# A chunked recurrence on one core: GpSimd's masked copies in one-input steps, the output norm at the end of its chunk, one transpose for two sources

## The reference

```python
def step(carry, inp):
    W1c, b1c = carry
    xq, xk, xv, et = inp
    Z1 = xk @ W1c + b1c
    grad = _ln_l2_bwd(Z1, xv - xk, g, bb)        # backward of a layer norm
    Attn1 = jnp.tril(xq @ xk.swapaxes(-1, -2))
    b1_bar = b1c - jnp.tril(et) @ grad
    Z1_bar = xq @ W1c - et * Attn1 @ grad + b1_bar
    last_eta = et[..., -1, :, None]
    W1n = W1c - (last_eta * xk).swapaxes(-1, -2) @ grad
    b1n = b1c - (last_eta * grad).sum(-2, keepdims=True)
    return ((W1n, b1n), xq + _ln(Z1_bar, g, bb, EPS_IN))
_, out = jax.lax.scan(step, (W1_0, b1_0), (chunk(XQ), chunk(XK), chunk(XV), eta))
x = x + L0(_gn(x));  x = x + L1(_gn(x))
```

## Time and profile before

| | |
|---|---|
| device time, median of 3 executions | 696.14 us (694.52 to 696.18) |
| the profiled execution's own time | 696.66 us |
| its span in the trace | 694.9 us |
| busy of the span: TensorE, weight load, VectorE, ScalarE, GpSimd | 76%, 53%, 71%, 48%, 54% |
| instructions on GpSimd | 660 |

### The profile page before, as it was taken

How to read it: one execution, slowest core, us unless ns; L and a number is a source line. 1 busy time by engine, 2 the same in 40 slices (tenths; PEclk the granted TensorE clock), 3 DMA queues, 4 the chain that set the end, 5 groups by cost and what they waited for, 6 DMA issues and landing times. The chain is left out here.

```text
span 694.9 us, 30768 instructions
## 1 busy us (share of the span) xinstructions
PE 528.8 (76%) x12150; PEld 368.1 (53%) x12150; DVE 491.4 (71%) x1547; ACT 331.6 (48%) x1044; POOL 377.8 (54%) x660
## 2 busy tenths in 40 slices
PE   0498999994577777777777777777773899669996
PEld 0143343434467666666666666666773345255542
DVE  6357676664588999999999999999995367434340
ACT  0434432224255555555555555555555576353422
POOL 0368788773365655655666556556664475402222
PEclk9999999996555555555555555555555899979987
DMA  9001111115600000000000000000001500001112
GB/s 349 36 18 39 34 30 31 30 41 121 145 4 0 0 0 0 0 0 0 0 0 0 0 0 0 0 0 0 0 4 42 218 0 0 1 18 62 52 42 90
DMA packets 9851, 24.56 MB, mean 35 GB/s; under 512 B 1845, under 2 KB 2510, under 8 KB 9550
## 3 DMA queue, kind: packets, MB, share of 16 engines
q1 hardware_dynamic: 9806, 24.01, 11.3%
HBM read 11.42 MB, written 4.19 MB: 22 GB/s over the span
## 5 line engine op out<-in xcount | busy, mean ns | idle before, releaser
L762 PE MATMUL PS<-work 32*32 32x32 f32 x4064 | 84.2, 238 | 76.1 <-DVE work L911 67.6
L762 PEld LDWEIGHTS PS<-work 32*32 32x32 f32 x4064 | 80.3, 152 | 86.2 <-issue 82.1
L963 POOL TENSOR_TENSOR work<-work,mask 128x256 f32<-128x256 f32 x64 | 46.7, 729 | 83.4 <-DVE work L911 70.6
L751 PE MATMUL PS<-work 64*32 64x64 f32 x2048 | 69.3, 310 | 19.3 <-ACT work L1006 17.1
L500 PE MATMUL PS<-X,work 128*128 (+3 forms) x160 | 72.1, 597 | 7.0 <-ACT X L640 6.4
L751 PEld LDWEIGHTS PS<-work 64*32 64x32 f32 x2048 | 55.6, 164 | 26.1 <-issue 24.8
L774 PE MATMUL PS<-work 32*64 32x32 f32 x2016 | 68.4, 292 | 0.6 <-issue 0.6
L774 PEld LDWEIGHTS PS<-work 32*64 32x64 f32 x2016 | 59.7, 216 | 4.8 <-issue 0.7
L1031 ACT ACTIVATE work<-PS,small 128x128 f32<-128x128 f32 x64 | 23.5, 367 | 80.1 <-PE PS L751 80.1
L1323 POOL TENSOR_TENSOR TT<-TT,KN 128x512 f32<-128x512 f32 x16 | 19.8, 1264 | 60.4 <-ACT TT L1454 60.2
L500 PEld LDWEIGHTS PS<-X,work 128*128 128x128 f32 (+1 forms) x160 | 25.9, 169 | 48.0 <-issue 47.1
(11 more groups left out here) (145 smaller groups left out, 1321.8 us busy)
## 6 DMA issues: line engine op xcount, KB each, us to landing
X<-in_x SPq DMA_DIRECT2D x4, 1024.0 KB, 8.1
KN<-KP SPq DMA_DIRECT2D x64, 64.0 KB, 1.9
X<-QP SPq DMA_DIRECT2D x8, 512.0 KB, 9.4
KN<-in_x SPq DMA_DIRECT2D x4, 1024.0 KB, 8.8
out<-TT SPq DMA_DIRECT2D x16, 256.0 KB, 2.2
work<-in_rope SPq DMA_DIRECT2D x2, 512.0 KB, 9.7
cst<-in_consts SPq DMA_DIRECT2D x1, 289.0 KB, 4.9
work<-in_wk SPq DMA_DIRECT2D x1, 256.0 KB, 11.1
```

The costliest lines, as they stand in the source:

```text
L751: mm = nc.tensor.matmul(PS[HD * a:HD * a + HD, ZB[p], b * ZW:b * ZW + ZW], KT2[p][r:r + 64, k * B + b, :, :].rearrange("p e t -> p (e t)") ...
L762: mm = nc.tensor.matmul(PS[HD * a:HD * a + HD, bank, b * width:b * width + HD], AM[p][HD * a:HD * a + HD, b, part, :, :].rearrange("p e t ...
L963: nc.gpsimd.tensor_tensor(AM[p].rearrange("p b s e t -> p (b s) e t"), S1[p].unsqueeze(2).broadcast_to([P, 2 * B, E, CS]), mask2.rearrange ...
```

## The change

The change is confined to the recurrence, apart from addresses. GpSimd's masked copies `KT2` and `KHX`, until now one two-input product each against a broadcast mask, become two one-input products each, with one column of the mask as the scalar. `out_norm(c-3)` moves from between `YL` and the wait for `GL` to the end of GpSimd's `body(c)`. The pair of variance and deviation `vq` gets two buffers. TT and KN become the halves of one tensor `TK`, so that VectorE's two transposes become one. GpSimd's chunks are all written out, where 56 of them ran in a loop. VectorE's `out_rows` with its wait is untouched.

```diff
-        KN = sb("KN", [P, J, NT])
-        TT = sb("TT", [P, J, NT])
+        TK = sb("TK", [P, J, 2, NT])
+        TT, KN = TK[:, :, 0, :], TK[:, :, 1, :]
...
-        vq = carve(2 * B)
-        var1, sdq = vq[:, 0:B], vq[:, B:2 * B]
+        vq = [carve(2 * B) for _ in range(2)]
+        var1, sdq = [v[:, 0:B] for v in vq], [v[:, B:2 * B] for v in vq]
...
                     if past(c, 2):
                         dve.wait_ge(q["khx"], c - 1)
-                    for s, src in enumerate((TT, KN)):
-                        tr = nc.vector.transpose(
-                            TKH[p][:, s, :, :].rearrange("p b d -> p (b d)"),
-                            src.rearrange("p e (b n) -> p b e n", b=B)[:, :, :, ds(c * CS, CS)])
-                    tr.then_inc(q["tkh"], 1)
+                    nc.vector.transpose(
+                        TKH[p].rearrange("p s b d -> p (s b d)"),
+                        TK[:, :, :, :].rearrange("p e s (b n) -> p (s b) e n", b=B)[:, :, :, ds(c * CS, CS)]
+                    ).then_inc(q["tkh"], 1)
...
                     if past(c, 2):
                         pool.wait_ge(q["base"], c - 1)
-                    nc.gpsimd.tensor_tensor(
-                        KT2[p], chunk(KP, c).unsqueeze(2).broadcast_to([P, J * B, E, CS]),
-                        ccol("emask_k").unsqueeze(1).unsqueeze(3).broadcast_to([P, J * B, E, CS]),
-                        ALU.mult).then_inc(q["kt2"], 1)
+                    for e in range(E):
+                        kt = nc.gpsimd.tensor_scalar(KT2[p][:, :, e, :], chunk(KP, c), ccol("emask_k", e, 1),
+                                                     None, ALU.mult)
+                    kt.then_inc(q["kt2"], 1)
...
-                    nc.gpsimd.tensor_tensor(
-                        KHX[p], TKH[p][:, 1, :, :].unsqueeze(2).broadcast_to([P, B, E, HD]),
-                        upd_mask.unsqueeze(1).unsqueeze(3).broadcast_to([P, B, E, HD]), ALU.mult
-                    ).then_inc(q["khx"], 1)
+                    for e in range(E):
+                        kx = nc.gpsimd.tensor_scalar(KHX[p][:, :, e, :], TKH[p][:, 1, :, :],
+                                                     upd_mask[:, e:e + 1], None, ALU.mult)
+                    kx.then_inc(q["khx"], 1)
...
                     nc.gpsimd.tensor_tensor(YL, YY[:, 0, :, :], bc(lead[:, 0, :]), ALU.mult).then_inc(q["yl"], 1)
-                    if past(c, 3):
-                        out_norm(c - 3, 1 - p)
                     pool.wait_ge(q["gl"], c + 1)
...
                     if not is_last(c):
                         khx(c + 1, 1 - p)
+                    if past(c, 3):
+                        out_norm(c - 3, 1 - p)
...
-                run_chunks(pool, body)
+                for c in range(NC):
+                    body(c, c % 2)
...
-                def out_sd(c):
+                def out_sd(c, p):
                     act.wait_ge(q["ssq"], c + 1)
-                    if past(c, 1):
-                        act.wait_ge(q["zn"], c + 0)
-                    nc.scalar.activation(sdq, ssq, ACT.Sqrt, bias=eps6, scale=1.0 / HD).then_inc(q["sdq"], 1)
+                    if past(c, 2):
+                        act.wait_ge(q["zn"], c - 1)
+                    nc.scalar.activation(sdq[1 - p], ssq, ACT.Sqrt, bias=eps6, scale=1.0 / HD).then_inc(q["sdq"], 1)
```

More of the change, by code:

```diff
@@ L851, in out_r @@
                     dve.wait_ge(q["sdq"], c + 1)
-                    nc.vector.reciprocal(sdq, sdq).then_inc(q["rq"], 1)
+                    o = 1 - c % 2
+                    nc.vector.reciprocal(sdq[o], sdq[o]).then_inc(q["rq"], 1)
                 def out_turn(c):
@@ L887, in body @@
                         dve.wait_ge(q["sdq"], c - 2)
-                        nc.vector.reciprocal(vq, vq).then_inc(q["r"], 1)
+                        nc.vector.reciprocal(vq[p], vq[p]).then_inc(q["r"], 1)
                     else:
-                        nc.vector.reciprocal(var1, var1).then_inc(q["r"], 1)
+                        nc.vector.reciprocal(var1[p], var1[p]).then_inc(q["r"], 1)
                     dve.wait_ge(q["ts"], c + 1)
@@ L970, in out_norm @@
                         pool.wait_ge(q["zt"], c + 0)
-                    nc.gpsimd.tensor_tensor(ZN, ZQ[p], bc(sdq), ALU.mult).then_inc(q["zn"], 1)
+                    nc.gpsimd.tensor_tensor(ZN, ZQ[p], bc(sdq[1 - p]), ALU.mult).then_inc(q["zn"], 1)
                 def body(c, p):
                     pool.wait_ge(q["r"], c + 1)
-                    nc.gpsimd.tensor_tensor(lead[:, 0, :], var1, lrh[:, ds(c, 1), :].squeeze(1), ALU.mult
+                    nc.gpsimd.tensor_tensor(lead[:, 0, :], var1[p], lrh[:, ds(c, 1), :].squeeze(1), ALU.mult
                                             ).then_inc(q["u"], 1)
                     pool.wait_ge(q["u"], c + 1)
-                    nc.gpsimd.tensor_tensor(lead[:, 1, :], var1, lead[:, 0, :], ALU.mult).then_inc(q["u2"], 1)
+                    nc.gpsimd.tensor_tensor(lead[:, 1, :], var1[p], lead[:, 0, :], ALU.mult).then_inc(q["u2"], 1)
                     pool.wait_ge(q["y"], c + 1)
                     nc.gpsimd.tensor_tensor(YL, YY[:, 0, :, :], bc(lead[:, 0, :]), ALU.mult).then_inc(q["yl"], 1)
-                    if past(c, 3):
-                        out_norm(c - 3, 1 - p)
                     pool.wait_ge(q["gl"], c + 1)
@@ L1058, in body @@
                         act.wait_ge(q["u2"], c + 0)
-                    nc.scalar.activation(var1, ss, ACT.Identity, bias=eps6, scale=1.0 / HD).then_inc(q["v"], 1)
+                    nc.scalar.activation(var1[p], ss, ACT.Identity, bias=eps6, scale=1.0 / HD).then_inc(q["v"], 1)
                     if past(c, 1):
@@ L1069, in body @@
                     if past(c, 2):
-                        out_sd(c - 2)
+                        out_sd(c - 2, p)
                     if past(c, 1):
@@ L1085, in _ @@
                 out_store(NC - 4)
-                out_sd(NC - 2)
+                out_sd(NC - 2, 0)
                 out_square(NC - 1, 1)
                 out_store(NC - 3)
-                out_sd(NC - 1)
+                out_sd(NC - 1, 1)
                 out_store(NC - 2)
@@ L1266, in build @@
             if at[1] + n > J * NT:
-                at = [flat(TT), 0]
+                at = [TT[:, 0, :], 0]
             DST.append(at[0][:, at[1]:at[1] + n].rearrange("p (r w) -> p r w", w=kept))
@@ L1273, in build @@
                for k, (r, w, _, kept) in zip((0, 1, 2, 0, 1), STAGES)]
-        YB = [flat(TT)[:, 4096 + s * 2048:4096 + (s + 1) * 2048].rearrange("p (k n) -> p k n", k=PER * J)
+        YB = [TT[:, 1, s * 2048:(s + 1) * 2048].rearrange("p (k n) -> p k n", k=PER * J)
               for s in range(2)]
```

## The result

The changed kernel takes 856.77 us (median of 4, 854.7 to 858.1) against 695.33 us for the kernel before, a ratio of 1.232 with a 95% interval of 1.228 to 1.235. It is slower, as forecast, but by 161 us, not by 86: the time lies 49 us above the range. It stands next to the rival in which each half costs as much as the whole, 858 us, to which I gave 6 in 100.

The account below looks back on a forecast made before the run. VectorE's program was taken as the bound, so new waits are paid in full. A chunk of 2.81 + 1.14 + 3.03 = 6.98 us against 5.55 gave 86.2 us more in all, so 782 us; range 766 to 808.

Parts of the forecast that it names:

- the rival in which each half costs as much as the whole: GpSimd's one-input steps each keep the halved product's 0.61 us through a fixed cost: 76 us more, 858 us; 6 in 100.
- The wait at `out_rows`: VectorE's `out_rows` waits for the moved norm, starting 2.81 us after the gradient instead of 0.63: about 2.2 us stall per chunk.
- the price of the one-input steps: GpSimd's four one-input steps per chunk each take 0.25 us to the next start, like the copy.
- The upper bound: A one-input step on GpSimd costs at most the same-size two-input product, 0.40 us, some 0.355 to the next start: +25 us.
- The part beside VectorE: From L874 to the next gradient VectorE takes 3.03 us instead of 3.48, as GpSimd is silent beside it.
- the written-out program: GpSimd starts its masks 0.37 us after the gradient instead of 0.51, counted within the wait; extra instruction fetch costs nothing.
- the single transpose: One VectorE transpose for two, between gradient and `out_rows`, is worth nothing with or without the new wait.
- the second buffer of the variances: ScalarE's `out_sd` waits for a norm one chunk older, off the path before and after: costs nothing.
- Nothing outside the recurrence: Changed addresses keep transfers' row lengths, so the stages outside the recurrence change by nothing.
- The rule on shared reads: A two-SBUF-input VectorE instruction and a GpSimd instruction reading SBUF exclude one another; without it the total is 27 us more.

Follow-up runs that it names:

- experiment 1: The changed kernel with the output norm back at its old place, ahead of the wait for the gradient: 687.59 us, ratio 0.988.
- experiment 8: The changed kernel with two-input products and the norm directly behind the masks, halfway between old and new place: 705.18 us, ratio 1.012.
- experiment 2: The changed kernel with each masked copy as one two-input product again, norm still at the end: 785.62 us, ratio 1.130.
- experiment 5: The changed kernel with eleven extra GpSimd instructions on scratch ahead of the recurrence, at 4, 128 or 256 elements: 859.81 us (one execution).
- experiment 6: The changed kernel with five extra GpSimd instructions ahead of the recurrence, of other operations, a strided view and a larger product: 857.43 us (one execution).
- experiment 7: The changed kernel with a second operation, an addition of 0.0, in each one-input step: 800.64 us, ratio 1.151.
- experiment 4: The kernel before with GpSimd's program written out and nothing else: 687.16 us, ratio 0.985.
- experiment 3: The changed kernel with the norm at its old place and two-input products: 684.52 us, ratio 0.984.
- experiment 9: The changed kernel with two-input products, a third buffer of ZQ and ScalarE's program written out, norm at the end: 687.27 us, ratio 0.985.
- experiment 10: The changed kernel with a third buffer of ZQ and ScalarE's program written out, one-input steps kept: 751.48 us, ratio 1.077.
- experiment 11: The changed kernel with two-operation one-input steps, third buffer of ZQ and ScalarE's program written out, norm at the end: 707.22 us, ratio 1.016.
- experiment 14: The changed kernel with third ZQ buffer, ScalarE written out, norm behind the masks, key blocks two-input, key rows one-input: 684.09 us, ratio 0.984.
- experiment 13: The changed kernel with the norm at its old place, key blocks one-input, key rows by a two-input product: 684.21 us, ratio 0.984.

## Why the prediction was right about the place and wrong about the size

*The wait at `out_rows`: right.* The wait that no row of before showed, with 1.28 us to spare, became 3.49 us of idle time in each chunk, released by L971, and in the last two chunks `out_rows` came 2.74 and 0.88 us after the gradient, the same sum with fewer terms. Experiments 1 and 8 move the wait with the norm's place, 8 hits 1.56 us exactly, and 2 hits 2.93 within 0.01.

*The step that failed is the price of the one-input steps: "The copy is the nearest row, with the same 128 elements per partition and one input, so I take 0.25 for each of the four."* A step measured 0.61 us, or 0.57 to 0.58 to the next start. Four times 0.32 more is 1.3 us a chunk, less 0.1 by which ScalarE and VectorE were quicker afterwards: 59 x 1.23 = 73 us, which with 782 gives 855. The upper bound was at fault too. I took the two-input product of the same size, 0.40 us, as the most that a product of one input could cost; the runs showed that one input can cost more than two. The rival that named 0.61 had the right number for a wrong reason, since no fixed cost rules: 4 elements take 0.30 us with a column, 128 take 0.61, 256 take 0.93. That its 858 us lie so near the measured 857 is luck in so far.

*Why the step is so long.* Experiments 5 to 7 show that it is the form with a single operation. With a second one that adds zero the same step takes 0.38 us, and the changed kernel 801 us, which lies inside my range. The 85 ns by which it is still above the copy are about the mask column's extra. Why the single form is slower inside GpSimd was not tried and stays open.

*The part beside VectorE: right, but not followed far enough.* From L874 to the gradient 3.03 was forecast and 3.01 came. Of the written-out program the prediction counted the 0.14 us by which the masks start sooner, and only as a part of the wait. Where there is no wait it is worth about 10 us (experiment 4): the earlier start shifts GpSimd's products against L870 and L902, which fall from 530 to 394 and from 366 to 306 ns.

*Nothing for the single transpose and the second buffer of the variances: right*, as far as the noise of 0.3 to 0.4% can tell (experiments 3 and 4). *Nothing outside the recurrence: right.* The first L870 starts at 168.6 us in both kernels, and from the last gradient to the end of the span it is 165.9 us before and 166.3 after.

*The second consumer of the norm.* The prediction named the count of `out_rows` only. L857, `out_turn(c-4)`, takes the norm of chunk c-4; in the kernel before that norm had ended at 401.17, 3.59 us before L857 started:

```profile
404.76 0.29 DVE L857 STREAM_TRANSPOSE work<-work 128x128 f32<-128x128 f32 x1
```

Experiments 9 to 11 show that L857 waits for the norm as well and binds as soon as the first wait is gone. In the changed kernel it is hidden, since `out_rows` has waited for the same norm in the chunk before.

*The rule on shared reads.* The Trainium skill ("SBUF — State Buffer", section "Who interferes with whom") has the second instruction to issue blocked until the first is through. With two-input products the rows agree: L870 takes 748 ns in experiment 14 and L884 577 in experiment 13, each ending 0.15 us after the product beside it. Beside one-input steps of 0.6 us L870 takes 291 and L876 280 in experiment 13, so there the measurement goes against full blocking.

## What to carry to other kernels

Before an instruction is moved past a wait, list every wait for its semaphore by count, with the slack that each has in the trace; a wait with slack has no row, and here two consumers on VectorE had one each, of 1.28 and 3.59 us. Bound the price of an instruction form that the trace lacks by a probe, or else widely: fewer inputs or fewer operations is no upper bound. Where instructions of two engines slow each other, look at what runs beside what before you look at how busy either engine is. In this kernel key rows that took GpSimd twice as long made it 13 us faster, and a collision that was moved onto another line was no gain.

## What was unexpected of the hardware

- On GpSimd a product of 128 elements per partition with a constant takes 528 ns, a product with an addition behind it 298 ns, a copy 292 ns, a product of two inputs 401 ns. The single-operation form costs 2.5 ns an element, the copy 0.85.
- A scalar taken from a column in memory adds 74 to 83 ns to it, at 4, 128 and 256 elements alike.
- A GpSimd program written out instead of looped took up the gradient 0.37 us after its start instead of 0.51, and that alone made the kernel 1.5% faster.
